# Identity matmuls in the waits of TensorE, and an expert's first projection issued one step earlier

## The reference

```python
x = _layernorm(x + _L0_attn_ref(x, ...))        # 16 heads: correlations, fitness weights, softmax
x = _layernorm(x + _L0_xattn_ref(x, ctx, ctx, ...))   # banded cross-attention, 16 heads of 16
x = _layernorm(x + _L0_ffn_ref(x, ...))         # quantised 256x256 projection
x = _layernorm(x + _L1_attn_ref(x, ...))        # moving average (convolution), gated attention
x = _layernorm(x + _L1_xattn_ref(x, ctx, ctx, ...))   # cross-attention, 16 heads of 64
x = _layernorm(x + _L1_ffn_ref(x, ...))         # 8 experts, top 2, 256 -> 1024 -> 256
```

## Time and profile before

| | before |
|---|---|
| time, median of 3 runs (lowest, highest) | 2370.12 us (2365.3, 2372.94) |
| time of the profiled execution, and its span | 2369.09 us, 2367.3 us |
| TensorE busy, matmuls | 2166.2 us (92%), 16842 |
| VectorE, ScalarE, GpSimd busy | 1326.0, 1122.7, 921.3 us |
| mean granted TensorE clock over the span | 0.967 of full |

### The profile page before, as it was taken

One profiled execution on the slowest core, in us unless ns is written; L12 is line 12 of the kernel. 1 busy time (PEld: TensorE's weight loads), 2 busy tenths in 40 slices (PEclk: granted clock), 3 DMA queues, 4 the chain that ended last, 5 costly groups with the idle time before them and its releaser, 6 DMA issues. The chain is left out here.

```text
span 2367.3 us, 44182 instructions
## 1 busy us (share of the span) xinstructions
PE 2166.2 (92%) x16842; PEld 1729.4 (73%) x16842; DVE 1326.0 (56%) x2511; ACT 1122.7 (47%) x1931; POOL 921.3 (39%) x962
## 2 busy tenths in 40 slices
PE   8899996899978999999998899999995999999993
PEld 6788775566655667666776688888874888888893
DVE  6899994899985910045556478888783111111113
ACT  5778784577665645343332455555552111111113
POOL 4787874445554930001101234444452222222222
PEclk8999998999999999999999899999997999999997
DMA  6345653111105795731211323333324756666564
GB/s 179 84 117 140 170 144 92 37 37 54 55 19 185 244 265 194 230 102 36 72 41 41 129 90 108 110 112 116 107 86 186 237 178 180 187 189 192 180 209 153
DMA packets 197376, 312.93 MB, mean 132 GB/s; under 512 B 62512, under 2 KB 173872, under 8 KB 183856
## 3 DMA queue, kind: packets, MB, share of 16 engines
q1 hardware_dynamic: 176960, 254.92, 33.7%
q0 software_dynamic: 13440, 17.90, 4.2%
q10 hardware_dynamic: 6768, 37.29, 4.0%
HBM read 188.62 MB, written 121.45 MB: 131 GB/s over the span
## 5 line engine op out<-in xcount | busy, mean ns | idle before, releaser
L2794 ACT ACTIVATE dec_area<-me_ps_h 128x512 f32<-128x512 f32 (+1 forms) x160 | 88.8, 555 | 422.9 <-PE me_ps_h L2772 422.9
L2835 DVE TENSOR_SCALAR me_yo<-me_ps_y,moe_xg 128x256 f32<-128x256 f32 x72 | 34.8, 484 | 428.5 <-PE me_ps_y L2782 409.5
L2703 POOL DMA_INDIRECT xo<-me_yo,me_row x72 | 112.8, 1567 | 409.9 <-DVE me_yo L2835 356.4
L2237 POOL TENSOR_TENSOR l1x_e<-l1x_e,l1x_ri 128x1024 f32<-128x1024 f32 x64 | 121.8, 1903 | 239.1 <-DVE l1x_ri L2497 239.1
L2772 PE MATMUL me_ps_h<-me_xt,me_w 128*128 128x256 f32 (+1 forms) x1056 | 210.0, 357 | 0.0
L2782 PE MATMUL me_ps_y<-me_w,dec_area 128*128 128x256 f32 x944 | 209.2, 379 | 0.7 <-DVE me_yo L2835 0.7
L2782 PEld LDWEIGHTS me_ps_y<-me_w,dec_area 128*128 128x128 f32 x944 | 178.7, 190 | 25.1 <-issue 1.1
L2772 PEld LDWEIGHTS me_ps_h<-me_xt,me_w 128*128 128x128 f32 x1056 | 181.7, 190 | 20.2
L898 POOL TENSOR_TENSOR l0x_e<-l0x_e,l0x_ri 128x1024 f32<-128x1024 f32 x64 | 120.1, 1897 | 151.1 <-DVE l0x_ri L1145 151.1
L2336 PE MATMUL l1x_ps_p<-l1x_xct,dec_area 128*128 128x256 f32 x512 | 127.0, 394 | 1.0 <-ACT l1x_xct L2422 1.0
L2435 ACT ACTIVATE l1x_e<-l1x_sx 128x1024 f32<-128x1024 f32 x64 | 67.5, 1055 | 116.3 <-DVE l1x_sx L2488 116.2
(11 more groups left out here) (428 smaller groups left out, 5377.1 us busy)
## 6 DMA issues: line engine op xcount, KB each, us to landing
me_w<-in_w SPq DMA_DIRECT2D x33, 2048.0 KB, 9.3
xs<-dec_zero SPq DMA_DIRECT2D x31, 1032.0 KB, 6.8
k<-kv_kt ACTq DMA_DIRECT2D x16, 1024.0 KB, 4.5
v<-kv_va ACTq DMA_DIRECT2D x16, 1024.0 KB, 4.6
l1x_kt<-k SPq DMA_DIRECT2D x16, 1024.0 KB, 5.0
l1x_va<-v SPq DMA_DIRECT2D x16, 1024.0 KB, 5.6
moe_w_first<-in_w SPq DMA_DIRECT2D x7, 2048.0 KB, 9.5
moe_xg<-xs SPq DMA_DIRECT2D x32, 258.0 KB, 2.8
```

Of the source, the lines that this page charges most:

```text
L2237: pool.tensor_tensor(e[:, n % 2, u, :, :], e[:, n % 2, u, :, :], spread(ri[:, n % 2, u, :], P), ALU.mult).then_inc(e_scaled, 1)
L2703: pool.indirect_dma_start(token_rows, bass.IndirectOffsetOnAxis(row[:, j % 2, q:q + 1], 0), yo[:, j % 2, q, :], None, compute_op=ALU.add). ...
L2794: act.activation(h[:, j % 2, 2 * i:2 * i + 2, 0:P * size(j)], ps_h[i % HB][:, :, 0:P * size(j)], ACT.Gelu).then_inc(gelued, 1)
```

## The change

A helper issues `count` matmuls of the identity with itself into a PSUM buffer that nobody reads at that moment. It is called at ten places of TensorE's programs; each call stands in the order of the engine like any other step. In `moe_experts` two entries of the step list change places.

```diff
+def busy(pe, out, ident, count):
+    for _ in range(count):
+        pe.matmul(out, ident[:, :], ident[:, :], start=True, stop=True)
...
 # l0_attn, tensor
+                def warm(count):
+                    busy(pe, ps_e[0][:, 0, :], ident, count)
+                def warm_late(count):
+                    item_done(pe, v_copied, TILES - 1)
+                    busy(pe, ps_a[1][:, 0, :], ident, count)
-                walk([(3, multiply), ..., (0, project_v), (2, lambda n: transpose_e(n, 2)), ..., (2, apply), (-1, transposes), (-1, lambda n: score(n, 0))])
+                walk([(3, multiply), ..., (0, project_v),
+                      at_step(0, lambda: warm(20)), at_step(1, lambda: warm(10)), (2, lambda n: transpose_e(n, 2)), (1, sum_inverse), ..., (0, lambda n: score(n, 1)), (2, apply),
+                      at_step(TILES - 1, lambda: warm_late(7)), at_step(TILES, lambda: warm_late(7)), at_step(TILES + 1, lambda: warm_late(5)),
+                      at_step(-1, lambda: warm(12)), at_step(1, lambda: warm(10)), (-1, transposes), at_step(0, lambda: warm(6)), (-1, lambda n: score(n, 0))])
+                item_done(pe, corr_done, 2 * TILES - 1)
+                busy(pe, ps_s[:, 0, 0, 0, :], ident, 26)
 # l0_xattn, end of tensor
+                item_done(pe, ot_copied, TILES - 1)
+                busy(pe, ps_e[0][:, 0, :], ident, 15)
 # mega_conv, end of tensor
+                pe.wait_ge(activated, CH // 4)
+                busy(pe, ps[0][:, 0, :], ident, 13)
 # mega_attn, end of tensor
+                item_done(pe, et_copied, NG - 1)
+                busy(pe, ps_s[:, 0, :], ident, 39)
 # l1_xattn, tensor
+                def warm(count):
+                    item_done(pe, shifted, 2 * TILES - 1)
+                    busy(pe, ps_s[:, 0, 0, :], ident, count)
-                     part(project_q, 3) + [(1, lambda n: apply(n, 1))])
+                     part(project_q, 3) + [(1, lambda n: apply(n, 1)), (TILES + 1, lambda n: warm(14 if n == 0 else 9) if n < G + 1 else None)])
+                warm(50)
 # moe_experts, tensor
-                unrolled(GROUPS, [(0, transposes), (1, up), (2, down_)])
+                unrolled(GROUPS, [(1, up), (0, transposes), (2, down_)])
```

More of the change, by code:

```diff
@@ L701, in multiply @@
                     last.then_inc(multiplied, 1)
-                walk([(3, multiply), (2, lambda n: transpose_e(n, 0)), (2, lambda n: transpose_e(n, 1)), (0, project_v), (2, lambda n: transpose_e(n, 2)), (1, sum_inverse), (2, lambda n: transpose_e(n, 3)), (0, lambda n: score(n, 1)), (2, apply), (-1, transposes), (-1, lambda n: score(n, 0))])
+                def warm(count):
[3 more added lines that the diff above has]
+                    busy(pe, ps_a[1][:, 0, :], ident, count)
+                walk([(3, multiply), (2, lambda n: transpose_e(n, 0)), (2, lambda n: transpose_e(n, 1)), (0, project_v),
+                      at_step(0, lambda: warm(20)), at_step(1, lambda: warm(10)), (2, lambda n: transpose_e(n, 2)), (1, sum_inverse), (2, lambda n: transpose_e(n, 3)), (0, lambda n: score(n, 1)), (2, apply),
+                      at_step(TILES - 1, lambda: warm_late(7)), at_step(TILES, lambda: warm_late(7)), at_step(TILES + 1, lambda: warm_late(5)),
+                      at_step(-1, lambda: warm(12)), at_step(1, lambda: warm(10)), (-1, transposes), at_step(0, lambda: warm(6)), (-1, lambda n: score(n, 0))])
+                item_done(pe, corr_done, 2 * TILES - 1)
+                busy(pe, ps_s[:, 0, 0, 0, :], ident, 26)
             @block.scalar
@@ L1649, in l0_ffn, with mega_conv @@
         kit.clear_semaphores()
-def mega_conv(nc, xn, kv, cv, mw, mx_out):
+def mega_conv(nc, ident, xn, kv, cv, mw, mx_out):
     G, CH = cv.G, cv.CH
@@ L2969, in decoder_stages @@
         mw = GatedAttentionInput(nc, stack, {k[1:]: v for k, v in t.items() if k[0] == "m"})
-        mega_conv(nc, xn, kv, cv, mw, mx)
+        mega_conv(nc, ah.ident, xn, kv, cv, mw, mx)
         mega_attn(nc, x3, xn, mx, ah, kv, cv, mw, x4)
```

## The result

The changed kernel takes 2363.39 us (median of 11 runs, 2356.50 to 2367.26), the kernel before 2370.12 (11 runs, 2365.30 to 2374.33). The ratio is 0.9975, with a 95% interval of 0.9964 to 0.9985: 0.25% faster. The gain is small, but the interval leaves 1 out, and a repeat gave 0.9979. The prediction said 2363.

A forecast was written before the change was run, and what follows sets the result against it. TensorE, busy 92% of the span, was taken to bound the expert stage. Terms -2.5 - 1.9 - 0.3 - 0.8 - 1.0 - 0.5 = -7.0 us took 2369.09 to 2362.1, or 2363 against the median; range 2353 to 2374.

The forecast's parts named there:

- The ramp: Fillers at the first stage's start (12, 20, 6, 10, 10): between -4.2 and +3.2 us, taken -2.5.
- the experts: Reordered steps let up(0) start 2.7 us earlier; weights for up(1) limit the gain: 0 to -1.1 us, taken -1.0.
- the tail: First stage's end: transposes and last multiply, run warm, save 1.1 and 1.0 us; together taken as -1.9.
- the end of `mega_attn`: 39 fillers at this stage's end: 4.2 us long, hidden in a wait of 10.87 us, so costing nothing.
- what shifts: First-stage stall on issue, read as late instructions: may go (-5.6 us) or another hit (+5.6); taken -0.5.
- Price of one identity matmul: For every filler: priced like a 128x128 float32 transpose, 0.11 us at full clock or 0.21 at half.
- the 1.0 that I had put on score(0, 1): In the first stage's start, this score call, run warm between ACT's tanh and VectorE's correlation, gives back 1.0 us.
- Other stage ends: Fillers ending `l0_xattn`, `mega_conv`, `mega_attn`, `l1_xattn` (15, 13, 39, 50): all hidden by the closing store or scatter.
- The -0.3 for `mega_attn`: At this stage's start, part of its 16 transposes may stay warm: 0 to -1.7 us, taken -0.3.
- The last routes: Fillers (14, 9) in waits of the final chain warm the last route and transposes: 0 to -1.4 us, taken -0.8.
- the branch for a cold up(0): At the experts' start, up(0) at half clock delays transposes(1) and its copy; up(1) starts about 1824.3: nothing gained.

The follow-up runs named there:

- the writes moved: First-stage 1 MB zero writes to the experts' slots issued in `l0_xattn` instead: kernel before 2361.07 us, changed kernel 2353.79; an earlier placement with 14 `mega_attn` fillers 2374.05.
- half the length: Changed kernel with every filler cut to half its matmuls, rounded up: 2360.22 us; with the zero writes also moved to `l0_xattn`, 2356.86.
- with transposes: Changed kernel with each filler matmul replaced by two transposes of the identity: 2365.50 us, ratio 0.998.
- the kernels with 14: Changed kernel with 14 identity matmuls, not 39, ending `mega_attn`: 2362.63 us; with zero writes moved to `l0_xattn` as well, 2374.05 and, placed better, 2354.17.

## Why the prediction was right, and where it wasn't

**The total.** 2363 against 2363.39; -7.0 us against -6.86 in the profiled executions. The ramp and the experts were right in size; the tail, the end of `mega_attn` and what shifts were off by 2.2 to 3.0 us each and, with smaller differences in other stretches, happened to cancel. That part is luck.

**Price of one identity matmul: the step that failed.** "An identity matmul has the same shape and I price it at 0.11 or 0.21 us." The rows it came from were of transposes, one pass each; a matmul of float32 is two. All fillers were twice as long as I thought (0.23 us each). The count was there to be read: `project_v` issues two matmuls and its row in the trace says x4.

**The ramp: -2.5 forecast, -2.82 measured** (-2.86 with the writes moved). The parts were read rightly, but one expectation failed. "I expect the clock to be lost again once in this ramp" did not happen: with twice the length, the waits are covered, and in all nine traces with the full ramp fillers the clock is 1.00 and tiles 0 and 2 are 20.0 us apart. With half the length, the length I had in mind, the clock is lost again in both traces, and the ramp takes 34.99 and 35.83 us, 0.9 and 1.7 more than the 34.1 of the full length. Of the gain 0.92 us lie between the two correlations of tile 0, so the 1.0 that I had put on score(0, 1) is there. The trace with half the length, cold at just this score and warm at the transposes ahead of it, has none of it. 1.92 lie between tiles 1 and 2 (I had 1.6), which stand 9.56 us apart and not 11.48; tiles 0 and 1 stay 10.44 apart (I had counted 0.5).

**The tail: -1.9 forecast, +1.05 measured.** The last multiply is warm as said, but a stall of 1.94 us that the kernel before doesn't have stands ahead of it (2.21 in the repeat and with transposes). The kernel before has no stall in its tail and takes 28.88 us; the five traces with tail fillers and no stall take 26.88 to 27.06, 1.8 to 2.0 less, as forecast. The five without tail fillers scatter from 28.03 to 30.40, by where the clock falls, so against the kernel before with the zeros moved it is -3.35. The mechanism and the size were right, and a term I had not put there hid them.

**What shifts: -0.5 forecast, -2.72 measured.** I read the 2.44 us as "instructions that were not there yet". The stall in tile 6 is in all eight traces that have the writes of zeros in the first stage and not the half length, at nearly the same instruction, 2.29 to 3.11 us long. In three it costs 2.3 to 3.0 us, in five 3.8 to 5.8: the latter are those in which the clock falls as it stands or right behind it. Before and after, from 114 us on:

```profile
114.00:118.00 4.00, 3.50 (x44) 2.97 (x48) 2.78 (x3) 1.89 (x3) 0.97 (x1) 0.69 0.01 4
118.00:122.00 4.00, 4.00 (x28) 3.31 (x21) 2.72 (x5) 1.62 (x3) 3.40 (x6) 0.50 0.00 0
```

```profile
114.00:118.00 4.00, 4.00 (x40) 3.53 (x34) 1.93 (x5) 3.26 (x6) 3.21 (x5) 1.00 0.00 0
118.00:122.00 4.00, 3.98 (x105) 3.50 (x104) 3.72 (x9) 2.90 (x5) 3.94 (x7) 1.00 0.02 6
```

That difference, 3.0 us between tiles 5 and 8, is the whole of the -2.72, and no filler stands within 49 us of it. I had foreseen that the stall can go or another hit, and had no way to say which. Only the half-length edit moved the stall to another tile, where it cost 0.95.

**Other stage ends: "All hidden" failed for the 39.** They last 8.87 us, not 4.2, and cost 2.4 to 2.7; hidden were 15, 13 and 26 calls. Nor was all of the 10.87 us there to hide in: as 8.87 us of fillers move SyncE's first issue by 12.30 - 9.87 = 2.43, some 6.4 us of it lie ahead of the stage's end (an estimate), and the rest is the next stage's load. Seven kernels start `l0_xattn` at half clock and take 313.5 to 314.7 us to its last multiply, five start it warm and take 313.3 to 315.3: no gain, so 0 was right. The -0.3 for `mega_attn` isn't there: to its last bias matmuls it takes 294.09 us, and 293.86 before. The 1.25 us between `l0_ffn` and `mega_conv` I can't assign: kernels without fillers at its start show 138.0 to 140.2 us, kernels with them 137.5 to 140.8.

**The last routes: -0.8 forecast, -1.6 measured** from first score to the experts, when the clock holds; of these 1.26 lie behind the last tile's exponentials (19.78 us to the last count, now 18.52). When the clock falls at the last route it is +0.6 to +1.4 against the kernels without fillers. **The experts: -1.0 forecast, -1.24 measured**, though 3.4 us of up(0) are cold. Seven runs that have the new order and 4.3 to 5.7 us of up(0) at half clock take 20.0 to 20.7 us to the first down-projection, against 20.3: the branch for a cold up(0) holds.

**The sum without the stalls.** Between the two kernels with the writes moved the terms are: start +0.94, ramp -2.86, tail -3.35, `mega_attn` +2.36, `l1_xattn` -2.03, experts -1.17, `l0_ffn` -1.34, the rest +0.04: -7.4 us, and 7.3 by the medians. The tail's -3.35 is against the slowest of the cold tails, and the start's +0.94 and the -1.34 of `l0_ffn` are scatter that no edit explains, so it is a rough figure. In the kernel as it was, a gain in one stall and a loss in another left nearly the same.

**Still open:** why the kernels with 14 lose the clock at the last route and those with 39 don't, three out of three and four out of four; up to the last tile's exponentials the two kinds run alike, 0.2 to 0.4 us apart. It is not the 39 that hold it: the kernel without any filler at the end of `mega_attn` keeps the clock at the last route too (first score to last count 476.47 us, as with 39), and then takes 1.2 us longer from there to the experts. And the half-length edit moved the stall as fewer matmuls ahead of it would (last part), but no run changed their number alone.

## What to carry over

Count a matmul's passes in the trace (the x behind the row) before pricing it, and size each filler to its wait also for the case that the clock is at half: where it ends last, it is the new bound. In the ramp, waits covered nearly whole gave 2.8 us and waits covered by half 1.1 to 1.9. And before gaining microseconds by warmth, look for a stall "on issue" and for a large transfer that nobody waits for beside it: moving one that was on no critical path gave as much or more (9.6 us) than some 240 added matmuls and a new order (6.7, and 7.3 without the stalls), as long as it was not put ahead of a store that ends a stage.

## What the runs showed of the hardware

**TensorE's stalls on issue and the large writes.** The DMA of the changed kernel at 109 to 110 us, right in the stall, and what had been issued between 104 and 109 us:

```profile
q1 hardware_dynamic: 193, 0.04, 23.6%
q8 instruction: 1, 0.02, 5.9%
```

```profile
xs<-dec_zero SPq DMA_DIRECT2D x1, 1032.0 KB, 7.1
toep<-l0a_kp SPq DMA_DIRECT2D x1, 32.0 KB, 6.8
```

From 100 to 109 us there is no packet of the instruction queue. One of 16 KB goes from 109.06 on, once the 1 MB is nearly through, and TensorE, which stopped at 109.03, resumes at 111.86. The 32 KB write behind the 1 MB takes 6.8 us to land (6.5 is the median of all 32 in this kernel); with the zeros moved the 32 such writes take this (median):

```profile
toep<-l0a_kp SPq DMA_DIRECT2D x32, 32.0 KB, 1.9
```

That moving the writes removes the stalls is shown, in five kernels (the longest left in the first stage is 0.49 us). That the instruction packet waits in the DMA engines behind the write is read from these rows, and not tested by itself.

Why most tiles, with the same write, have no stall can be read from how many matmuls TensorE has done when it stops. Up to the stall of tile 6, in the kernel before and in the changed one (PE's count is the first in brackets):

```profile
0.00:112.06 112.06, 96.12 (x1080) 81.66 (x1080) 84.05 (x129) 69.70 (x99) 63.99 (x109) 0.88 0.50 139
...
0.00:109.03 109.03, 98.38 (x1208) 86.04 (x1208) 84.14 (x129) 69.03 (x99) 63.90 (x109) 1.00 0.52 143
```

In every trace with the five full ramp fillers, and the writes where they were, the stall comes after exactly 1208 passes, in both traces without fillers after 1080. The other stalls over 0.3 us stand at set distances too: within each group of kernels with the same fillers in the ramp, 41 stalls in nine traces are multiples of 123.45 passes apart, to within 1.3. The instruction queue moves one 16 KB packet about as often: 42, in the changed kernel 43, in the first 380 us, in which the trace has 5229 and 5392 passes. So a stall stands where one packet is used up and the next is late, and a tile is spared when no such place falls into its write. That also gives a reading of what the fillers did to the stall: the 116 passes in the ramp are nearly one packet, so it came back almost where it had been; 58 are half of one, and it came two tiles earlier. This is an account that fits all nine traces, not an experiment on the count.

Whether the clock falls behind such a stall is not settled by its length: it fell in five traces at 2.44 to 3.11 us, and stayed up in three at 2.29 to 2.83.
